# A recurrent layer's weights loaded late in 32x32 blocks and turned by VectorE, one late tile of x loaded behind the first rows

## The reference, cut to what matters

```python
# x: 8 sequences x 512 steps x 256 channels, f32; cond: 8 x 256
def moe(x, cond):                        # 8 experts, the best 2 of each token, one shared unit
    shared = silu(x @ w1) * (x @ w3) @ w2
    s = sigmoid(concat(x, cond) @ router_W)
    routed = sum over the 2 best experts of gate * (gelu(x @ W1e) @ W2e)
    return (shared + routed) / 3

def gru(X, h0):                          # h0 = cond
    Xz, Xr, Xh = X @ Wxz.T + bxz, X @ Wxr.T + bxr, X @ Wxh.T + bxh
    for t in range(512):
        Z = sigmoid(Xz[t] + H @ Whz.T + bhz)
        R = sigmoid(Xr[t] + H @ Whr.T + bhr)
        H = Z * H + (1 - Z) * tanh(Xh[t] + (R * H) @ Whh.T + bhh)
        Y[t] = H @ Whq.T + bhq
x = x + moe(x, cond)
x = x + gru(x, cond)
```

## Time and profile before

| what | value |
|---|---|
| median of 3 runs | 1282.59 us (1282.32 to 1283.2) |
| span of the profiled execution | 1282.1 us |
| own time of that execution | not recorded apart from the span; the median stands 0.49 us above the span |
| instructions | 84275 |
| PE busy | 1255.5 us, 98% of the span |
| DVE busy | 996.5 us, 78% |
| ACT busy | 805.1 us, 63% |
| POOL busy | 7.4 us, 1% |
| mean granted TensorE clock | 0.998 of full speed |
| first instruction of scan step 0 on PE | 50.99 us from the span's start |

### The profile page before, as it was taken

The page is one execution under the profiler, slowest core; times in us unless marked ns, Lnnn a source line. Parts: engine busy times, 40 slices in busy tenths (PEclk is TensorE's granted clock), DMA queues, the critical chain, the costliest instruction groups (busy, mean ns, idle before and its releaser), DMA issues.

```text
span 1282.1 us, 84275 instructions
## 1 busy us (share of the span) xinstructions
PE 1255.5 (98%) x35592; PEld 879.3 (69%) x35592; DVE 996.5 (78%) x6111; ACT 805.1 (63%) x4402; POOL 7.4 (1%) x25
## 2 busy tenths in 40 slices
PE   9999999999999999999999999999999999999887
PEld 8876667766667766667767666766666766666554
DVE  6678787787787878778787887777877787877765
ACT  4366666666666666666666666666666666666554
POOL 1000000000000000000000000000000000000000
PEclk9999999999999999999999999999999999999999
DMA  9311011111101111011111101111011111000110
GB/s 272 59 33 44 23 40 27 42 40 34 39 20 42 35 37 45 24 37 27 43 40 34 38 21 43 33 38 45 27 33 27 44 39 33 23 21 26 33 32 11
DMA packets 76185, 51.34 MB, mean 40 GB/s; under 512 B 40608, under 2 KB 73760, under 8 KB 75808
## 3 DMA queue, kind: packets, MB, share of 16 engines
q1 hardware_dynamic: 75128, 45.29, 13.9%
q10 hardware_dynamic: 680, 0.66, 0.2%
HBM read 29.13 MB, written 16.78 MB: 36 GB/s over the span
## 4 chain that ended last, share of the span: by engine, by line
PE 93%; DVE 3%; ACT 2%; issue 1%; DMA 1%; SPq 0%
PE dn_ps L1073 27%; PE up_ps L1100 26%; PE zc_bank L1235 21%; PE r_bank L1235 15%; PE aux L1073 2%; DVE terms L996 2%; PE dn_ps L1107 1%; ACT t_h L705 1%; PE misc L1073 1%; DVE hist L999 1%; DMA x_all<-in_x 1%; ACT t_r L685 0%; DVE t_rT L974 0%; PE zc_bank L1048 0%; DVE rhT L977 0%
## 5 line engine op out<-in xcount | busy, mean ns | idle before, releaser
L974 DVE STREAM_TRANSPOSE t_rT<-t_r 128x32 f32<-128x32 f32 x1024 | 156.1, 191 | 176.6 <-ACT t_r L685 167.4
L685 ACT ACTIVATE t_r<-r_bank 128x32 f32<-128x32 f32 x1024 | 146.3, 195 | 213.9 <-PE r_bank L1235 201.5
L705 ACT ACTIVATE t_h<-zc_bank 128x32 f32<-128x32 f32 x1024 | 146.1, 195 | 208.2 <-PE zc_bank L1235 208.2
L1073 PE MATMUL dn_ps<-we_sb,x_all 128*32 128x256 f32 (+1 forms) x5144 | 274.8, 329 | 0.0
L1235 PEld LDWEIGHTS zc_bank<-whT,rhT 128*8 128x8 f32 x8192 | 118.2, 87 | 177.9 <-DVE rhT L977 176.9
L1235 PE MATMUL r_bank<-whT,hist 128*8 128x64 f32 x8192 | 210.1, 220 | 16.6 <-DVE hist L999 13.6
L1235 PE MATMUL zc_bank<-whT,rhT 128*8 128x64 f32 x8192 | 211.5, 220 | 2.7 <-DVE rhT L977 0.3
L1235 PE MATMUL zc_bank<-whT,hist 128*8 128x64 f32 x8192 | 208.9, 219 | 0.4 <-issue 0.4
L1235 PEld LDWEIGHTS r_bank<-whT,hist 128*8 128x8 f32 x8192 | 117.8, 88 | 111.5 <-DVE hist L999 92.7
L996 DVE STREAM_TRANSPOSE terms<-t_h 128x32 f32<-128x32 f32 x1024 | 156.5, 192 | 39.6 <-ACT t_h L705 20.7
L1073 PEld LDWEIGHTS dn_ps<-we_sb,x_all 128*32 128x32 f32 x5144 | 138.2, 110 | 31.0
(11 more groups left out here) (132 smaller groups left out, 1663.8 us busy)
## 6 DMA issues: line engine op xcount, KB each, us to landing
gate_inputs_by_group<-gru_raw SPq DMA_DIRECT2D x64, 192.0 KB, 2.0
gru_raw<-gate_inputs_by_group SPq DMA_DIRECT2D x256, 48.0 KB
xT_all<-in_x SPq DMA_DIRECT2D x448, 8.0 KB
x_all<-in_x SPq DMA_DIRECT2D x31, 128.0 KB
out<-gru_raw SPq DMA_DIRECT2D x31, 128.0 KB
x_all<-in_L_cond_W1e SPq DMA_DIRECT2D x4, 512.0 KB, 7.5
we_sb<-in_L_cond_W2e SPq DMA_DIRECT2D x4, 512.0 KB, 8.4
xT_all<-in_L_cond_w SPq DMA_DIRECT2D x2, 256.0 KB, 5.6
```

Of the source, the lines that this page charges most:

```text
L685: act.activation(t_r[:, i, :], r_ps[:, i * Q:(i + 1) * Q], ACT.Tanh, scale=0.5).then_inc(tr_ready, 1)
L705: act.activation(t_h[:, i, :], c_ps[:, i * Q:(i + 1) * Q], ACT.Tanh, scale=-1.0).then_inc(th_ready, 1)
L974: dve.transpose(t_rT[:, i, :], t_r[:, i, :]).then_inc(trT_done, 1)
L1073: done = pe.matmul(ps[Q * j:Q * (j + 1), col:col + cols], lhsT[:, Q * j:Q * (j + 1)], rhs, start=first, stop=last, tile_position=(0, Q * j ...
```

## The change

Each recurrent weight is no longer loaded by one DMA in rows of 1 KB. It is loaded by four DMAs (one for each column group j), each into 32 partitions, so that 32x32 blocks lie where a block transpose of VectorE turns them into place. An input weight goes in pieces of 128 bytes, 512 pieces a DMA (`load_wx`, 12 DMAs); a state or output weight in pieces of 256 bytes, 256 pieces a DMA (`load_blocks`, 16 DMAs). All 28 stand on SP behind the six gate biases and ahead of `bias_q`. The state weights' blocks lie in tiles 6 to 13 of `x_all`. VectorE turns them with 6 and 8 transposes of 128x256 elements. TensorE's seven groups, their evacuation and GpSimd's copies go. ScalarE halves `whT` of the candidate once, between `consume_up(1, 0)` and `consume_up(1, 1)`. `load_late(4)` moves from ahead of `store_inputs(0, 0)` to behind the second `gate_rows`.

```diff
@@ SP
-            for r, part, _ in WEIGHTS:
-                if part == "x":
-                    load_gru(r, ld_gru_x)
             load_we1(2)
             load_we2(1)
-            for r, part, _ in WEIGHTS:
-                if part != "x":
-                    load_gru(r, ld_gru_h)
             load_we1(3)
...
+            def load_blocks(blocks, w, loaded):
+                by_row = w.rearrange("(n r) c -> r n c", r=Q)
+                for j in range(NG):
+                    sp.dma_start(blocks[Q * j:Q * (j + 1), :, :], by_row[:, :, GW * j:GW * (j + 1)]).then_inc(loaded, 16)
+            def load_wx(g):
+                by_row = gru_wx[g].rearrange("(n r) (k c) -> r k n c", r=Q, k=KC)
+                for j in range(NG):
+                    sp.dma_start(wx_blocks[g][Q * j:Q * (j + 1), :, :, :], by_row[:, :, :, Q * j:Q * (j + 1)]).then_inc(ld_wx[g], 16)
...
                     sp.dma_start(dst[:, gate, :], src.rearrange("(a c) -> a c", a=1).to_broadcast([P, C])).then_inc(ld_bias, 16)
+            for g in range(GATES):
+                load_wx(g)
+            sp.wait_ge(shared_ready, 2)
+            for g in range(GATES + 1):
+                load_blocks(wh_blocks[g], gru_wh[g], ld_wh[g])
             sp.dma_start(bias_q[:, :], bhq.rearrange("(a c) -> a c", a=1).to_broadcast([P, C])).then_inc(ld_bias, 16)
-            load_late(EARLY)
...
                 gate_rows(q, 1, xs_second)
+            load_late(EARLY)
             load_late(EARLY + 1)
@@ GpSimd
-            pool.wait_ge(ld_gru_h, LDH)
-            for r, w in ordered.items():
-                for o in range(KC):
-                    pool.tensor_copy(...).then_inc(ordered_done, 1)
-            pool.wait_ge(tr_done, WEIGHTS_DONE)
+            pool.wait_ge(wx_turned, GATES * KC)
             pool.memset(xs, 0.0).then_inc(xs_zeroed, 1)
@@ ScalarE
-                take_round(e)
...
             consume_up(1, 0)
+            act.wait_ge(wh_turned, GATES * NI)
+            act.activation(whT[:, 2, :, :], whT[:, 2, :, :], ACT.Copy, scale=0.5).then_inc(whh_halved, 1)
             consume_up(1, 1)
@@ VectorE
+            def turn_wx(g):
+                dve.wait_ge(ld_wx[g], 16 * NG)
+                for k in range(KC):
+                    dve.transpose(wxT[:, k, :, COLS[g]].rearrange("p j (b r) -> p j b r", r=Q),
+                                  wx_blocks[g][:, k, :, :].rearrange("p (j b) q -> p j b q", j=NG)).then_inc(wx_turned, 1)
+            def turn_wh(g):
+                dve.wait_ge(ld_wh[g], 16 * NG)
+                for i in range(NI):
+                    dst = whT[:, g, i, :] if g < GATES else wqT[:, i, :]
+                    dve.transpose(dst.rearrange("p (n r) -> p n r", r=Q), wh_blocks[g][:, :, Q * i:Q * (i + 1)]).then_inc(wh_turned, 1)
...
-                if e > 2:
-                    take_round(e)
                 accumulate(0, e - 1)
+                if e >= NE - GATES:
+                    turn_wx(e - NE + GATES)
...
             accumulate(1, 0)
-            for q in range(PIECES):
-                add_bias(0, q)
+            turn_wh(0)
+            add_bias(0, 0)
+            turn_wh(1)
+            add_bias(0, 1)
+            turn_wh(2)
             shared_silu(1, 0)
             shared_hidden(1, 0)
+            turn_wh(3)
             shared_silu(1, 1)
@@ TensorE
                 unit(0, NSH + e)
-                downs = [(0, e)]
-                for at in range(max(len(ROUND_TR[e]), len(downs))):
-                    if at < len(ROUND_TR[e]):
-                        transposes(m)
-                        m += 1
-                    if at < len(downs):
-                        whole_down(*downs[at])
+                whole_down(0, e)
...
+                    if (t, q) == (0, 0):                     # project
+                        pe.wait_ge(wx_turned, GATES * KC)
...
+                        pe.wait_ge(wh_turned, NI * (GATES + 1))   # output, tile 0
...
                             pe.wait_ge(seeded_r, 1)
+                            pe.wait_ge(wh_turned, NI * 2)
+                            pe.wait_ge(whh_halved, 1)
```

More of the change, by code:

```diff
@@ L73, in moe_then_gru @@
         gru_raw = sb("gru_raw", [P, 11, KC, C])
-        raw = [gru_raw[:, r, :, :] for r in range(7)]
-        ordered = {r: gru_raw[:, 7 + i, :, :] for i, r in enumerate((1, 3, 5, 6))}
+        RB = C // Q
+        wx_blocks = [gru_raw[:, g, :, :].rearrange("p o c -> p (o c)").rearrange("p (k n q) -> p k n q", k=KC, q=Q) for g in range(GATES)]
+        BLOCK_HOME = 6
+        wh_blocks = [x_all[:, BLOCK_HOME + 2 * g:BLOCK_HOME + 2 * (g + 1), :].rearrange("p n c -> p (n c)").rearrange("p (n c) -> p n c", n=RB)
+                     for g in range(GATES + 1)]
         we2_sb = sb("we2_sb", [P, NE, HE // P, C])
@@ L151, in moe_then_gru @@
         ld_h0 = sem("ld_h0")
-        ld_gru_x = sem("ld_gru_x")
-        ld_gru_h = sem("ld_gru_h")
+        ld_wx = [sem(f"ld_wx{g}") for g in range(GATES)]
+        ld_wh = [sem(f"ld_wh{g}") for g in range(GATES + 1)]
+        wx_turned = sem("wx_turned")
+        wh_turned = sem("wh_turned")
+        whh_halved = sem("whh_halved")
         ld_bias = sem("ld_bias")
@@ L162, in moe_then_gru @@
         consts_ready = sem("consts_ready")
-        ordered_done = sem("ordered_done")
         tr_done = sem("tr_done")
@@ L225, in moe_then_gru @@
         EARLY = 4
-        WEIGHTS = [(0, "x", 0), (2, "x", 1), (4, "x", 2), (1, "h", 0), (3, "h", 1), (5, "h", 2), (6, "q", 0)]
-        WSCALE = {"x": [1.0, 1.0, 1.0], "h": [1.0, 1.0, 0.5], "q": [1.0]}
         HEAD_TR = [("x", 0), ("x", 1), ("cond", 0)]
[L230 to L234, removed]
+        NTR = len(HEAD_TR)
+        gru_wx = [wxr, wxz, wxh]
+        gru_wh = [whr, whz, whh, whq]
         gate_bx = [bxr, bxz, bxh]
         gate_bh = [bhr, bhz, bhh]
-        LDR, LDX, LDH = 16 * 3, 16 * 3, 16 * 4
+        LDR = 16 * 3
         LDB = 16 * (2 * GATES + 1)
@@ L243, in w13_cols @@
             return slice(half * HS // 2, (half + 1) * HS // 2)
-        def in_round(e):
-            sizes = [len(HEAD_TR)] + [len(r) for r in ROUND_TR]
-            return range(sum(sizes[:e + 1]), sum(sizes[:e + 2]))
         def evacuate(m):
-            kind, i = GROUPS[m]
+            kind, i = HEAD_TR[m]
             src = tr_ps[m % 2]
@@ L255, in evacuate @@
                 return xT_all[:, 2 * i:2 * i + 2, :, :].rearrange("p n k t -> p (n k t)"), src[:, 0:512], 1.0
[L256 to L259, removed]
-            if part == "x":
[L261 to L264, removed]
+            return condT[:, :, :].rearrange("p k t -> p (k t)"), src[:, 0:C], 1.0
         def sig(p):
@@ L554, in take @@
                 act.activation(dst, src, ACT.Copy, scale=s).then_inc(tr_act, 1)
[L556 to L560, removed]
             def score_tanh(i, tiles):
@@ L919, in _ @@
                 op()
-            take_round(2)
             for e in range(2, NE):
@@ L1035, in transposes @@
                     blocks = [x_all[:, 2 * i + n, k * P:(k + 1) * P] for n in range(2) for k in range(KC)]
-                elif kind == "cond":
+                else:
                     pe.wait_ge(ld_router, LDR)
                     blocks = [cond_tok[:, k * P:(k + 1) * P] for k in range(KC)]
[L1039 to L1044, removed]
-                    w = raw[r] if part == "x" else ordered[r]
-                    blocks = [w[:, o, k * P:(k + 1) * P] for k in range(KC) for o in range(KC)]
                 for at, blk in enumerate(blocks):
@@ L1179, in output @@
                 if i == 0:
+                    if t == 0:
+                        pe.wait_ge(wh_turned, NI * (GATES + 1))
                     pe.wait_ge(yst_ready, t + 1)
```

5 lines of the change are left out of this document (removed).

## The result

| | before | after |
|---|---|---|
| median | 1282.96 us (6 runs, 1282.32 to 1286.08) | 1295.78 us (6 runs, 1291.49 to 1301.10) |
| ratio | | 1.0097, 95% interval 1.0078 to 1.0116 |
| span of the profiled execution | 1282.1 us | 1295.5 us |
| mean granted clock | 0.998 | 0.994 |

The change makes the kernel 1% slower. The prediction was 1290.8 us with a range of 1281 to 1301: the time lies inside, 5 us above the forecast. One execution of the six, 1301.10 us, lies just above it. The profiled execution after took 1297.31 us, 1.8 us more than its span.

A forecast was written before the change was run, and what follows sets the result against it. Bound: TensorE's chain up to scan step 0. Wait for bias_q 5.4 (the 3.08 saving already counted) + transposes 0.1 + clock 1.5 + late tile 1.25 = 8.2 us on span 1282.1, giving 1290.3, median 1290.8; range 1281 to 1301.

The forecast's parts named there:

- the wait: Before the scan: the bias adds wait for bias_q behind the 28 block loads, delaying step 0 by 5.4 us.
- the stretch from there to step 0: Between the bias_q wait and step 0: 0.1 us for VectorE's transposes and 1.5 us for the lowered clock.
- the late tile: Behind step 4: VectorE waits 1.6 us for load_late(4), less 0.36 us idle; scan loses 1.25 us once, bounds 0 and 3.
- the likeliest case: Whole kernel: the wait for bias_q as forecast, landing between 40.5 and 49 us, 1284 to 1296 us; chance 0.61.
- slow issues: Rival on SP's queue: issuing grows with the pieces, 1.3 us for each of 12 loads, bias_q at 51.7, 1298.2 us; chance 0.15.
- the landing that costs nothing: Before the bias adds: bias_q landing at 38.95 us leaves step 0 as today; each microsecond later delays it by one.
- Landing of bias_q: Before the bias adds: bias_q issued at 41.2 us behind the 28 loads, landing 3.1 us later at 44.3 us.
- SP is what decides: Before the bias adds: SP's issuing sets bias_q's landing at 44.3 us; the DMA engines bound it from below at 40.5.
- Dear packets: Rival on the block loads: small packets cost 49 ns each under load, 26.4 us in all, 1309 us; chance 0.06.
- The clock: Behind TensorE's wait for bias_q: granted clock halves for 3.5 us, costing 1.5 us; bounds 0 and 1.75.
- VectorE's transposes: In the prologue: 0.42 us each; six count nothing, eight nearly fit gaps between adds, 0.1 us, at most 3.4.
- The gain: In the prologue: seven groups of four transposes leave TensorE's chain, 0.44 us each, 3.08 us, contained in the main term.

The follow-up runs named there:

- the last kernel: Changed kernel with bias_q first and load_late's 128 KB DMA first, plus the output weight's four block loads moved behind the first half of gate_rows: 1285.89 us, ratio 1.0030.

## Why the prediction was right

The mechanism was right and the sizes were short. Each of the three terms that made up the 8.2 us came out larger: the wait 6.4 us for 5.4, the stretch from there to step 0 2.2 for 1.6, the late tile 4.0 for 1.25. The median lies 0.2 us inside the likeliest case (1284 to 1296) and the range was wide towards the slow side for the sake of a rival, slow issues, which did not come; that it took in the larger late tile and the stalls of the scan is in part luck.

**Direction and main cause.** Right, and shown: moving bias_q alone takes 9.2 us out before the scan. The working put the landing that costs nothing at 38.95 us, from the end of VectorE's accumulate at 40.51. TensorE was itself busy until 40.85 us, so VectorE had 0.3 us to spare: a landing 6.75 us later delayed `transpose_x1(0)` by 6.4.

**Landing of bias_q.** Forecast 44.3 us, measured 45.7. SP began the blocks at 23.1 us (22.3): the last expert weight was issued by 17.4 us and not 15.8, and the six biases took 2.8 us and not 4.0. The 12 input loads took 0.91 us each (0.76), the 16 others 0.50 (0.61), the landing 3.5 us (3.1). The sizes erred both ways and left 1.4 us. "SP is what decides" holds: from 37 to 43 us the DMA engines were busy 58.6%, with SP issuing without a gap.

```profile
q1 hardware_dynamic: 3334, 0.81, 58.6%
```

That is 0.586 x 16 x 6 us / 3334 = 16.9 ns for a piece of some 240 bytes. The rival that issuing grows with the pieces is true in a small way: in steady issue 512 pieces took 0.63 us, 256 pieces 0.45. In the changed kernel nothing was seen of 1.3 us a load beyond 2.1 and 2.0 us on two single loads. But with the input blocks first, issued right behind the expert weights from 17.49 us on, the first five took 1.3 to 1.9 us each: long issues go with a busy stretch here, and for an earlier place of the loads the rival's price would have been the right one.

**Dear packets.** The Trainium skill (DMA: Bandwidth & Descriptors, Specifications) has line rate only from pieces of 512 bytes on. The trace agrees in direction: 240 bytes in 16.9 ns are 14 bytes per ns, against 21 for rows of 1 KB. The price of small pieces does not decide here, because the blocks come when the engines have room. Issued by GpSimd into the full stretch the loads do cost: 348 GB/s became 208 to 220. The price that I took from a quiet stretch would have misled for such an earlier place. Why these engines moved less, the pieces' size or GpSimd's queue beside SP's, was not told apart.

**The clock.** Forecast 1.5 us with a bound of 1.75, measured 2.0 by the kernel with TensorE kept busy. The low clock lasted from `transpose_x1(0)` until 51.4 us, 4.2 us of work and not 3.5.

**The late tile.** The worst-sized term: 1.25 us forecast, "once", with a bound of 3; 4.0 us measured. The place was right and the load's issue was as long as before (9.77 us for 16, begun as far behind step 0). But the wait was 3.05 us, not 1.6: the 128 KB load landed 4.2 us after its issue instead of 2.7. The slack of 0.36 us held, which makes 2.7 us. And behind the wait the clock fell again, which the sum had only for the first wait: the other 1.3 us. By itself, without the fall, the move costs 2.1 us.

**VectorE's transposes.** Rightly counted as almost nothing: 0.38 us each. With row loads TensorE ran dense past them from 25.4 us on, and the last bias add came 2.57 us earlier where `transpose_x1(0)` came 2.65: 0.1 us, as counted.

**The gain.** 3.08 us on TensorE are real as 2.65 us, since TensorE then waits once for VectorE's accumulate, which the forecast did not look at. At step 0 they are 2.4, since store and reload took 0.4 us longer and took over the end. The forecast put this chain 0.6 us ahead of TensorE's, by the start of the first seed (50.40 us); the seed takes 0.23 us more, so that only 0.3 us were to spare.

**What is left.** 6.4 us of wait, 2.2 us to step 0 behind it, and 4.0 us are 12.6 of the 13.4 us of span. The stalls of the scan add 2.0 us, and the fall of the clock near the end, which only the execution before had, takes 1.1 away.

## What to carry to other kernels

When loads are moved or split, count every instruction that the issuing queue now passes before the next load that someone waits for; here a 128 KB load of no hurry stood behind 28 others because it shared a semaphore count with loads that were in a hurry. A wait of TensorE can cost more than its length: behind the two waits here the work ran at half the clock for 4.2 and 3.2 us. And relieving the engine that sets the end pays only as far as the others keep up: here one wait for VectorE and a slower reload turned 3.08 us into 2.4.

## What the runs showed of the hardware that was not expected

- With block loads on GpSimd's queue beside SP's row loads, the 16 DMA engines were recorded as full (share 1.06 to 1.12) and moved 208 to 220 GB/s instead of 348.
- A 128 KB load of x, behind 16 small ones, landed 2.7 us after its issue in the kernel before and 4.2 us in the changed one (70.36 to 74.58 us). In the latter the next tile's small loads were issued right behind it; with the same loads behind it, it took 3.1 us in the kernel with bias_q first.
- The length of TensorE's wait did not tell by itself whether its clock fell. Behind step 4 it idled 2.00 us in the last kernel, and the clock then fell from 65.8 to 69.0 us; in the kernel before with the late tile moved it idled 2.10 us (until 66.29) and the clock stayed at 1.00. It fell behind 2.22, 2.45 and 2.58 us, and not behind 1.22 and 1.43. 8.3 us of idling brought 4.2 us of work at 1.2 GHz.
- TensorE stalled for 0.4 to 1.1 us amid a row of products with nothing recorded that it waited for, three times in the changed kernel's profile. The kernels of the experiments scatter by 1.3 to 9.2 us, against 5.1 for all executions of the kernel before; a wait behind step 4 does not sort them, since the kernel with the late tile by GpSimd, which has none, scatters by 6.9.
